# A decoder layer on one Trainium2 core: one rope product placed inside the layer-norm statistics, and the orders of the value projection, the cross-attention value product and the first transposes moved

## The reference

```
x = x + self_attn(layernorm(x))            # 16 heads of 32, rope on q and k, causal mask, Wo
x = x + cross_attn(layernorm(x), ctx)      # 32 heads of 16, axial rope on q and k from positions, Wout + bout
x = x + down(silu(gate(z)) * up(z))        # z = layernorm(x); weights (integer - 128) * scale, hidden size 1408
```

## Time and profile before

| | |
|---|---|
| median of 3 runs | 1677.6 us (1676.05 to 1678.58) |
| the profiled execution | 1680.36 us, of which its span (first to last instruction) 1678.5 us |
| busy, share of the span | PE 97%, PEld 76%, DVE 69%, ACT 58%, POOL 33% |
| mean granted TensorE clock | 0.993 of full |
| start of scores1 in turn 0, and in `last()` | 25.97 us, 1097.97 us |
| one loop turn, scores1 to scores1 | 34.73 to 34.77 us |

### The profile page before, as it was taken

How to read it: one execution, slowest core, us unless ns; L and a number is a source line. 1 busy time by engine, 2 the same in 40 slices (tenths; PEclk the granted TensorE clock), 3 DMA queues, 4 the chain that set the end, 5 groups by cost and what they waited for, 6 DMA issues and landing times. The chain is left out here.

```text
span 1678.5 us, 42062 instructions
## 1 busy us (share of the span) xinstructions
PE 1625.0 (97%) x15216; PEld 1267.4 (76%) x15216; DVE 1162.9 (69%) x2087; ACT 967.3 (58%) x3847; POOL 548.4 (33%) x535
## 2 busy tenths in 40 slices
PE   6899999999999999999999999998999999999997
PEld 4677777777777777777777777766888888888885
DVE  7788788888888888888888878786744344344332
ACT  5577677777777777777767777675422222222221
POOL 4344443444444444444444444341011011011011
PEclk9999999999999999999999999998999999999999
DMA  6011111111110011111111011022420120120110
GB/s 215 29 32 31 36 34 50 30 30 36 41 43 30 30 36 47 37 30 36 30 54 30 30 36 33 23 70 90 150 76 26 50 75 25 50 75 25 50 50 26
DMA packets 55098, 81.00 MB, mean 48 GB/s; under 512 B 4880, under 2 KB 25488, under 8 KB 55056
## 3 DMA queue, kind: packets, MB, share of 16 engines
q1 hardware_dynamic: 55056, 80.43, 14.7%
HBM read 63.63 MB, written 16.78 MB: 48 GB/s over the span
## 5 line engine op out<-in xcount | busy, mean ns | idle before, releaser
L949 ACT ACTIVATE prob<-bank,nmax 128x128 f32<-128x128 f32 x1536 | 539.9, 408 | 155.8 <-DVE nmax L1180 151.7
L949 ACT ACTIVATION_READ_ACCUMULATOR prob<-bank,nmax 128x1 f32 x1536 | 380.7, 248 | 0.0
L1588 PE MATMUL fbank<-shared,piece_hi 128*128 128x512 f32 x1152 | 280.3, 394 | 0.0
L1180 DVE TENSOR_REDUCE nmax<-bank 128x4 f32<-128x512 f32 x376 | 233.5, 683 | 64.8 <-PE bank L536 51.2
L1588 PEld LDWEIGHTS fbank<-shared,piece_hi 128*128 128x128 f32 x1152 | 215.8, 187 | 53.2
L399 POOL TENSOR_TENSOR rope_buf<-rope_buf 128x512 f32<-128x512 f32 x128 | 165.6, 1303 | 159.7 <-DVE rope_buf L1133 159.6
L1740 DVE SCALAR_TENSOR_TENSOR h<-fbank,su_c,sil 128x512 f32<-128x512 f32 x88 | 66.0, 750 | 200.1 <-PE fbank L1588 197.1
L1674 ACT ACTIVATE sil<-fbank,sg_c 128x512 f32<-128x512 f32 x88 | 60.5, 687 | 174.8 <-PE fbank L1588 172.2
L1680 ACT ACTIVATE h_h<-h 128x512 fp32r<-128x512 f32 x88 | 55.6, 632 | 175.1 <-DVE h L1740 175.1
L449 POOL TENSOR_TENSOR cn_l<-cn,cn_h 128x512 fp32r<-128x512 f32 x64 | 82.8, 1294 | 211.9 <-DVE cn L1172 211.9
L512 PE MATMUL bank<-shared,z1T_h 128*128 128x512 f32 x520 | 140.4, 412 | 4.5 <-ACT shared L932 2.6
(11 more groups left out here) (178 smaller groups left out, 3170.2 us busy)
## 6 DMA issues: line engine op xcount, KB each, us to landing
xA<-in_x SPq DMA_DIRECT2D x32, 256.0 KB, 3.1
xB<-in_x SPq DMA_DIRECT2D x32, 256.0 KB, 3.0
x_scratch<-x SPq DMA_DIRECT2D x32, 256.0 KB, 2.0
shared_loaded<-x_scratch SPq DMA_DIRECT2D x8, 1024.0 KB, 7.7
xr<-x_scratch SPq DMA_DIRECT2D x8, 1024.0 KB, 5.7
out<-xr SPq DMA_DIRECT2D x8, 1024.0 KB, 4.3
cx<-in_ctx SPq DMA_DIRECT2D x32, 128.0 KB, 2.2
range_window<-in_wg SPq DMA_DIRECT2D x27, 112.0 KB, 2.0
```

The lines of the kernel that those rows point to most:

```text
L949: last = nc.scalar.activation(prob[:, c, i, :], S[c][:, i * P:(i + 1) * P], ACT.Exp, bias=nmax[:, c, i:i + 1], accum_out=rs[:, h:h + 1])
L1180: nc.vector.tensor_reduce(out=nmax[:, c, :], in_=S[c][:, :].rearrange("p (g k) -> p g k", g=G), op=ALU.max, axis=AX, negate=True).then_inc ...
L1588: last = nc.tensor.matmul(dst[:, :], w[:, k, cols], z[:, k, :], start=(n == 0), stop=(n == len(passes) * KT - 1))
```

## The change

Four edits, all in the attention phase:

- DVE: `statistics` takes a function `between`, called after bn_stats and before the wait for it. `link` is split into `step` (count) and the wait, and `rope` into `rope_cos` and `rope_sin`. In turns with sq and cq, the cos product of k2's rope is now issued between bn_stats and bn_aggr of `statistics(2, ...)`; its sin product stays behind the row maxima of "2b", ahead of the rope of k1.
- DVE, turn 0 alone: the row maximum of bank 0 goes first, then z1T_low, then the maxima of the other three banks.
- PE, turns with cq: in `transpose_query_z1_and_probs`, P0 goes ahead of T1 and of the three waits, and P1 ahead of T2: P0 T1 P1 T2 P0' P1' for T1 P0 T2 P1 P0' P1'.
- PE: the first part of v1 goes ahead of attend2("2a") and has 9 products for 10 (`V1_SPLIT`); 3 are left behind the key transposes.

```diff
--- before.py
+++ after.py
@@ -609,15 +609,15 @@
 
             def transpose_query_z1_and_probs(sq, cq, nx):
                 tiles = ((PA, RA["q2"]), (PC, z1))
+                ready = [first_halves_of_probs("1", sq, 0)]
                 pe.wait_ge(rot["q2"], cq + 1)
                 pe.wait_ge(v1_r, sq + 1)
                 pe.wait_ge(z_r[1], nx + 1)
                 tiles_ready = first_halves_of_two(tiles)
-                ready = [first_halves_of_probs("1", sq, 0)]
+                ready.append(first_halves_of_probs("1", sq, 1))
                 q2, z = second_halves_of_two(tiles, tiles_ready)
                 q2.then_inc(rT_d["q2"], 1)
                 z.then_inc(zT_d[1], 1)
-                ready.append(first_halves_of_probs("1", sq, 1))
                 for pair in range(2):
                     second_halves_of_probs("1", pair, ready[pair])
 
@@ -658,7 +658,7 @@
                 transpose4(PC, columns(z1)).then_inc(zT_d[1], 1)
 
             V1_STEPS = [(a, w, j) for a, w in ((z1T_h, WHI["v1"]), (z1T_h, WLO["v1"]), (z1T_l, WHI["v1"])) for j in range(KT)]
-            V1_SPLIT = 10
+            V1_SPLIT = 9
 
             def project_v1(steps):
                 for n in steps:
@@ -784,13 +784,13 @@
                     scores2("2b")
                 if has_n and has_c:
                     project_k1(nx)
-                if has_c:
-                    pe.wait_ge(v2_r, cq + 1)
-                    attend2("2a")
                 if has_n:
                     if has_s:
                         pe.wait_ge(x1_r, sq + 1)
                     project_v1(range(V1_SPLIT))
+                if has_c:
+                    pe.wait_ge(v2_r, cq + 1)
+                    attend2("2a")
                 if has_s:
                     transpose_keys_and_probs(sq, cq, nx)
                 if has_n:
@@ -1085,18 +1085,25 @@
         def _(dve):
             small = {"n": 0, "base": 0}
 
-            def link(ins):
+            def step(ins):
 
                 small["n"] += 1
                 ins.then_inc(dstep, 1)
-                dve.wait_ge(dstep, small["base"] + small["n"])
+                return small["base"] + small["n"]
+
+            def link(ins):
+
+                dve.wait_ge(dstep, step(ins))
 
 
             def flat(t):
                 return t[:, :, :].rearrange("p k t -> p (k t)")
 
-            def statistics(n, tile, q):
-                link(nc.vector.bn_stats(st[n][:, :], tile[:, :]))
+            def statistics(n, tile, q, between=None):
+                done = step(nc.vector.bn_stats(st[n][:, :], tile[:, :]))
+                if between is not None:
+                    between()
+                dve.wait_ge(dstep, done)
                 dve.sem_inc(aggr, 1)
                 nc.vector.bn_aggr(mv[n][:, :], st[n][:, :]).then_inc(mv_r[n], 1)
                 dve.wait_ge(mv_r[n], q + 1)
@@ -1115,6 +1122,10 @@
                     .then_inc(z_r[n], 1)
 
             def rope(n, q, src, w, cos, sin, scale):
+                rope_cos(n, q, src, w, cos, scale)
+                rope_sin(n, src, w, sin, scale)
+
+            def rope_cos(n, q, src, w, cos, scale):
 
                 h = D // w
                 dve.wait_ge(pj[n], q + 1)
@@ -1130,6 +1141,10 @@
                 nc.vector.scalar_tensor_tensor(
                     out=RA[n][:, :].rearrange("p (h j) -> p h j", j=w), in0=src[:, :].rearrange("p (h j) -> p h j", j=w),
                     scalar=scale, in1=cos.to_broadcast([P, h, w]), op0=ALU.mult, op1=ALU.mult)
+
+            def rope_sin(n, src, w, sin, scale):
+
+                h = D // w
                 last = nc.vector.scalar_tensor_tensor(
                     out=RB[n][:, :].rearrange("p (h j e) -> p h j e", j=w // 2, e=2),
                     in0=src[:, :].rearrange("p (h j e) -> p h j e", j=w // 2, e=2)[:, :, :, ::-1], scalar=scale,
@@ -1315,13 +1330,15 @@
                     rope("q1", nx, PA, DK1, cos1, sin1, DK1 ** -0.5)
                     split_low(EARLY[2:])
                     rope("k1", nx, TC, DK1, cos1, sin1, 1.0)
-                if has_s:
-                    row_maxima("1", sq, range(G))
                 if is_first(sq):
+                    row_maxima("1", sq, (0,))
                     z1T_low(1)
+                    row_maxima("1", sq, (1, 2, 3))
                     split_low(["o1"])
                     rope("q1", nx, PA, DK1, cos1, sin1, DK1 ** -0.5)
                     first_copies()
+                elif has_s:
+                    row_maxima("1", sq, range(G))
                 if has_o:
                     context2(oq, PB)
                 if has_c:
@@ -1367,12 +1384,13 @@
                     even_copies("2a", cq)
                 if has_s:
                     dve.wait_ge(x1_r, sq + 1)
-                    statistics(2, x1A, sq)
+                    k2_cos = (lambda: rope_cos("k2", sq, TC, DK2, axial(sq)[0], 1.0)) if has_c else None
+                    statistics(2, x1A, sq, between=k2_cos)
 
                 if has_c:
                     row_maxima("2b", cq, range(G))
                 if has_s and has_c:
-                    rope("k2", sq, TC, DK2, *axial(sq), 1.0)
+                    rope_sin("k2", TC, DK2, axial(sq)[1], 1.0)
                 if has_n and has_s and has_c:
                     rope("k1", nx, PA, DK1, cos1, sin1, 1.0)
                 if has_s:
```

## The result

The changed kernel takes 1664.65 us (median of 4 runs, 1663.07 to 1665.93); the kernel before, beside it, 1677.84 (4 runs). The ratio is 0.9918, with a 95% interval of 0.9906 to 0.993: 13.2 us less, where 12.9 were forecast. The profiled execution took 1663.07 us, with a span of 1661.3.

What follows compares the result with a forecast made beforehand. PE, busy 97% of the span, was taken as the bound; 27 loop turns gave 11.9, turns 2 and 30 0.9, turn 1 -0.1, turn 0 +0.2: 1677.6 - 12.9 = 1664.7 us, 8-in-10 range 1660 to 1672.5.

Steps and rivals of the forecast that it cites:

- steps 1 and 2: Keys' T1: rope side allows 608.03 to 608.1 for 608.63, PE's new order 608.21, so T1 comes 0.42 us earlier.
- step 1: DVE's statistics: cos product delays bn_aggr 0.40 to 0.45 us, inside 0.46 idle; POOL's sums end at 607.92 to 608.0.
- step 3: From keys' T1 to scores1: the stall pays for the moved v1 product, gaining 0.36 to 0.42 us per turn, 0.40 taken.
- rival of a floor at the loop's end: Branch and register work, not DVE, make the 0.79 us from z2 transposes to scores1; 1671 us, 14% chance.
- step 4: Query stage: P0 fills a 0.20 us stall, but ACT's odd copies bind next; 0.13 gain to 0.06 loss, +0.04 taken.
- rival that ACT doesn't bind: In the query stage the full 0.2 to 0.26 us is kept each turn; 1659 us, 6% chance.
- step 5: Turn 1: P1 waits for exponentials, scores2("2a") 0.46 us later, key stage gains 0.33, net -0.13; turn 0 gains 0.2.

Runs made afterwards that it cites:

- e1: Kernel before with only the cos product of k2's rope moved between bn_stats and bn_aggr; ratio 1.0002.
- e2: Kernel before with only PE's order changed: nine v1 products ahead of attend2("2a"); ratio 1.0002.
- e3: Kernel before with the cos product move and PE's v1 order and split together, without the query order and turn 0's edit; ratio 0.9931.
- e6: Changed kernel with attend2("2a") put back ahead of v1, still split at 9; ratio 0.9955 to the kernel before.
- e8: Changed kernel with v1 split at 8, so four products behind the key transposes; median 1664.04 us.
- e10: Changed kernel with the copy of the transposed q2 made by DVE instead of ACT, ahead of its even copies; 1659.79 us.
- e7: Changed kernel with the old order of half steps in turn 1 alone; median 1662.93 us.
- e5: Changed kernel without its edit in turn 0, the four row maxima staying ahead of z1T_low; ratio 0.9915 to the kernel before.

## Why the prediction was right

- **T1 of the keys is held from two level sides** (steps 1 and 2): right, and shown by e1, e2 and e3. T1 came 0.42 earlier in its stage, to the hundredth. e6 puts the change of kind that goes at 0.20, for 0.19.
- **The cos product fits the idle time** (step 1): right. It pushed bn_aggr from 0.84 to 1.29 behind bn_stats, 0.45, and the row maxima not at all. The Trainium skill (VectorE: DVE Perf Modes, "The DRAIN you can't avoid") measured eight copies, where a semaphore after each "costs nothing extra". That does not carry over to this pair: with the wait alone 0.84, and the product between added 0.45, less than its own step of 0.60.
- **The moved product pays with the stall** (step 3): right; 3.24 from T1 to scores1. The rival of a floor at the loop's end was wrong: PE alone needs 0.52 and not 0.79, and as much without the loop (e8). What the straight code of turn 30 to `last()` took before, 0.62, was no floor either, since DVE's copies ended there at 1096.63 + 1.28 = 1097.91, 0.06 ahead of scores1.
- **The query stage** (step 4): right that ACT's odd copies are the next wait; the size was off, 0.15 for 0.04 and outside my bound of 0.13. The reading that scores2("2a") waited for ACT already in the kernel before was wrong: PE held it, with 0.31 from the copies' end. And I took the delay from a released wait to PE between 0.10 and 0.24; it is 0.09 here in the loop too, and T2 slipped by 0.07, the least that I had allowed. The 0.24 at scores1 is no measure of it. The rival that ACT doesn't bind is refuted by e10, where another 0.16 a turn comes free once ACT's chain is shorter.
- **Turn 1** (step 5): the term failed. The later scores2("2a") was seen (0.46 forecast, 0.51 measured), but not that TensorE's clock would fall behind the longer wait: the turn took 1.66 more where 0.13 more was forecast. In its place e7, and e3 beside e5, show 2.06 for the new order in this turn; the key stage gave 0.40 for 0.33 (e3).
- **Turn 0**: the edit is worth nothing, as forecast (e5).

So two errors partly cancel: the loop gave 15.3 us for 11.9, 3.4 more than forecast, and turn 1 lost 1.5 more. The terms measured in the timelines, 15.3 from the loop, 0.75 from turns 2 and 30, less 1.7, give 14.3 without turn 0, where the forecast had 12.7. The medians show 13.2, with an interval of about 11.7 to 15.8. That they come within 0.3 us of the forecast is luck; that the gain lies near 13 is not.

## What to carry to other kernels

Where an engine starts a step close behind a release and also just when its own work ends, no single edit moves it: look for both sides and move them together, and expect each alone to measure as nothing. When a step is moved ahead of a wait, ask who waits for what it is now in front of, and ask it again for the turns at the pipeline's start, where the work that covers it in the steady state isn't there. A forecast should be read term by term: its total can be right by cancellation.

## What the runs showed that I had not expected

- A wait of 1.71 us on PE where there had been one of 1.33 brought a stretch at 1.2 GHz behind it (granted clock 0.57 over 4 us), which cost 1.5 us, four times what the wait had grown by.
- PE idled 1.27 to 1.55 us once, in the loop's first pass, at the same instruction in three of twelve changed kernels, with no wait there. In these three alone, a transfer of instructions starts late, 1.0 to 1.5 us into the pass; that it is the cause isn't shown.
- The step from the z2 transposes to scores1 takes at least 0.52 us on PE, in the loop or out of it. What differs is the delay behind the last release: scores1 starts 0.24 us after DVE's copies end in a loop turn of the kernel before, 0.15 at the start of turn 30 and 0.06 in `last()`, both straight code. No run tells why.
